# A row of offsets is added by GpSimd to the residual rows instead of by a TensorE product with ones

## The reference, cut to what matters

```python
y  = layernorm(x)                                    # without gain
y  = layernorm(y + causal_attention(y, y, y), g1, beta1)
y  = layernorm(y + attention(y, ctx, ctx), g2, beta2)
ff = relu(y @ w1 + b1) @ w2 + b2                     # 256 -> 1024 -> 256
y  = layernorm(y + ff, g3, beta3)
x  = x + y
n  = layernorm(x)
h  = silu(fp4(n) @ fp4(w_gate).T) * (fp4(n) @ fp4(w_up).T)   # 256 -> 704
x  = x + fp4(h) @ fp4(w_down).T                      # 704 -> 256
```

## Time and profile before

| | |
|---|---|
| median of 3 runs | 696.39 us |
| the profiled execution | 696.67 us, of which the span of the trace is 694.9 us |
| busy: PE, PEld, DVE, ACT, POOL | 84%, 78%, 75%, 54%, 48% of the span |
| granted TensorE clock, mean | 0.95 of full speed |
| two slots in the steady part | 74.2 us |

### The profile page before, as it was taken

How to read it: one execution, slowest core, us unless ns; L and a number is a source line. 1 busy time by engine, 2 the same in 40 slices (tenths; PEclk the granted TensorE clock), 3 DMA queues, 4 the chain that set the end, 5 groups by cost and what they waited for, 6 DMA issues and landing times.

```text
span 694.9 us, 12367 instructions
## 1 busy us (share of the span) xinstructions
PE 583.9 (84%) x3989; PEld 542.1 (78%) x3989; DVE 517.9 (75%) x1305; ACT 376.3 (54%) x763; POOL 332.8 (48%) x444
## 2 busy tenths in 40 slices
PE   2744679998999989898989899998989898888665
PEld 1634568888898889897979898888989797878564
DVE  3966546878787887878787968788778878687662
ACT  2434526566565657474737565566657574646241
POOL 2332514465544555464646454555546554544431
PEclk9965979999999999999999999999999999999785
DMA  7320000001010101010100001010100010000000
GB/s 230 108 67 0 3 30 22 17 1 46 2 54 1 47 1 54 1 45 0 53 0 22 23 15 38 0 45 0 53 1 30 1 31 9 9 8 9 8 8 15
DMA packets 18726, 19.30 MB, mean 28 GB/s; under 512 B 1520, under 2 KB 18176, under 8 KB 18688
## 3 DMA queue, kind: packets, MB, share of 16 engines
q1 hardware_dynamic: 18688, 18.82, 8.9%
HBM read 14.62 MB, written 4.19 MB: 27 GB/s over the span
## 4 chain that ended last, share of the span: by engine, by line
PE 53%; DVE 21%; issue 11%; POOL 8%; ACT 4%; DMA 1%; SPq 1%; DVEq 0%; ACTq 0%; POOLq 0%
PE R L850 6%; PE R L851 5%; PE R L852 5%; POOL hq L448 5%; PE R L762 4%; DVE ha L1216 4%; PE R L915 3%; PE R L917 3%; PE R L916 3%; DVE hs L1210 2%; PE TR L762 2%; PE O L961 2%; PE O L959 2%; PE O L960 2%; DVE st L1153 2%
## 5 line engine op out<-in xcount | busy, mean ns | idle before, releaser
L436 POOL TENSOR_TENSOR rs<-mv,neg_half 128x1 f32<-128x1 f32 (+1 forms) x112 | 70.2, 635 | 79.1 <-DVE mv L1157 78.9
L850 PE MATMUL R<-gu_hi,xqT_hi 128*128 128x352 f32 x256 | 88.2, 344 | 5.4 <-ACT xqT_hi L596 2.2
L851 PE MATMUL R<-gu_lo,xqT_hi 128*128 128x352 f32 x256 | 83.1, 325 | 0.0
L852 PE MATMUL R<-gu_hi,xqT_lo 128*128 128x352 f32 x256 | 83.0, 324 | 0.0
L442 POOL TENSOR_TENSOR hs<-hh,h_rec 128x704 f32<-128x704 f32 x32 | 50.8, 1586 | 62.2 <-DVE h_rec L1193 62.2
L590 ACT ACTIVATE w_raw<-w_raw,nm,rs 128x256 f32<-128x256 f32 x64 | 36.6, 596 | 80.3 <-DVE nm L1163 80.3
L915 PE MATMUL R<-y2T_hi,w_hi 128*128 128x256 f32 x256 | 75.1, 293 | 3.3 <-DVE y2T_lo L1293 3.3
L959 PE MATMUL O<-w_hi,hT_hi 128*128 128x256 f32 x256 | 73.7, 288 | 0.0
L960 PE MATMUL O<-w_lo,hT_hi 128*128 128x256 f32 x256 | 72.8, 284 | 0.0
L961 PE MATMUL O<-w_hi,hT_lo 128*128 128x256 f32 x256 | 72.8, 284 | 0.0
L916 PE MATMUL R<-y2T_lo,w_hi 128*128 128x256 f32 x256 | 72.4, 283 | 0.0
(11 more groups left out here) (149 smaller groups left out, 1864.7 us busy)
## 6 DMA issues: line engine op xcount, KB each, us to landing
x_in<-in_x SPq DMA_DIRECT2D x16, 256.0 KB, 2.9
x_res<-in_x SPq DMA_DIRECT2D x16, 256.0 KB, 2.8
out<-x SPq DMA_DIRECT2D x32, 128.0 KB, 1.9
hT<-in_L_xattn_w SPq DMA_DIRECT2D x2, 1024.0 KB, 7.0
ctx_rows<-in_ctx SPq DMA_DIRECT2D x16, 64.0 KB, 2.5
wd_raw<-in_L_ffn_w_down SPq DMA_DIRECT2D x1, 704.0 KB, 11.4
w_raw<-in_L_ffn_w_gate SPq DMA_DIRECT2D x1, 640.0 KB, 5.2
w_raw<-in_L_ffn_w_up SPq DMA_DIRECT2D x1, 640.0 KB, 6.7
```

Source lines behind the costliest of these rows:

```text
L436: pool.tensor_tensor(rs[i][:, t0:t0 + len(ts)], mv[i][:, t0:t0 + len(ts), 1], neg_half[:, 0:len(ts)], ALU.pow).then_inc(ln_rstd[i], 1)
L850: mm(o, xh, gu_hi[:, c, m, cols], start=(c == 0), stop=False)
L851: mm(o, xh, gu_lo[:, c, m, cols], start=False, stop=False)
L852: last = mm(o, xl, gu_hi[:, c, m, cols], start=False, stop=(c == KC - 1))
```

## The change

POOL now makes y2 in two instructions for each half: z2 * g2 as before, and then, once its own first result is written, y2 = y2 + shift2_row in place. The second waits on a new semaphore y2_gained that the first raises; the consumers wait for y2_set as before, which the second raises. TensorE's product of ones and shift_parts is gone, and so are the tiles ones and shift_parts, two memsets on POOL, two ACT instructions of 1x256 and one of DVE at the start. The first of the three products of block 0 now starts the sum.

```diff
-            pool.memset(ones[:].bitcast(F32), 1.0).then_inc(const_set, 1)
-            pool.memset(shift_parts[:].bitcast(F32), 0.0).then_inc(const_set, 1)
-            pool.wait_ge(const_set, 5)
+            pool.wait_ge(const_set, 3)
...
+            def shifted_rows(b, h, t):
+
+                wait(pool, ln_out[2], b, h, F, T, t + 1)
+                pool.tensor_tensor(y2[:, t, :], z2[:, t, :], g2_row[:], ALU.mult).then_inc(y2_gained, 1)
+                wait(pool, y2_gained, b, h, F, T, t + 1)
+                if isinstance(b, int) and HALVES * b + h == F:
+                    pool.wait_ge(shift2_set, 1)
+                pool.tensor_tensor(y2[:, t, :], y2[:, t, :], shift2_row[:], ALU.add).then_inc(y2_set, 1)
...
-                    gain_rows(b, h, F, t, 2, z2, y2, g2_row, y2_set)
+                    shifted_rows(b, h, t)
...
-                        act.wait_ge(shift2_set, 1)
-                        for p in (0, 32):
-                            act.activation(shift_parts[p:p + 1, :], shift2_row[p:p + 1, :],
-                                           ACT.Copy).then_inc(shift_hi_set, 1)
...
                 o = O[1][:, 0:D]
-                if fs[0] == 0:
-                    mm(o, ones[:], shift_parts[:], start=True, stop=False)
                 for f in fs:
                     hi, lo = hT_hi[:, f, P * t:P * (t + 1)], hT_lo[:, f, P * t:P * (t + 1)]
-                    mm(o, hi, w2_hi[:, f, :], start=False, stop=False)
+                    mm(o, hi, w2_hi[:, f, :], start=(f == 0), stop=False)
...
-                        dve.wait_ge(shift_hi_set, 2)
-                        v.tensor_tensor(shift_parts[32:33, :], shift2_row[32:33, :], f32(shift_parts[32:33, :]),
-                                        ALU.subtract).then_inc(shift_parts_set, 1)
```

More of the change, by code:

```diff
@@ L103, in layer_program @@
         shift2_row = sb("shift2_row", [P, D])
-        shift_parts = sb("shift_parts", [P, D], F32R)
-        ones = sb("ones", [P, P], F32R)
         b1_fold = sb("b1_fold", [P, FC])
@@ L186, in layer_program @@
         ident_set = sem("ident_set")
-        shift2_set, shift_hi_set, shift_parts_set = sem("shift2_set"), sem("shift_hi_set"), sem("shift_parts_set")
+        shift2_set, y2_gained = sem("shift2_set"), sem("y2_gained")
         b1_turned, b1_fold_set = sem("b1_turned"), sem("b1_fold_set")
@@ L555, in _ @@
         def _(act):
-            act.wait_ge(const_set, 5)
+            act.wait_ge(const_set, 3)
             act.wait_ge(cols_turned, 1)
@@ L815, in weights_ready @@
                     pe.wait_ge(w1_lo_set, KC)
-                    for s in (w2_hi_set, w2_lo_set, b1_fold_set, shift_parts_set):
+                    for s in (w2_hi_set, w2_lo_set, b1_fold_set):
                         pe.wait_ge(s, 1)
```

## The result

The changed kernel takes 703.41 us, the median of 20 runs (699.42 to 705.79), against 697.44 us of the kernel before, the median of 20 runs beside it (695.56 to 699.81). The ratio is 1.0076, with a 95% interval of 1.0061 to 1.0092: 5.3 us slower by the ratio, 6.0 by the two medians. The forecast was +1.4 us on the 696.39 us then known, or 697.8. The measured time lies above the forecast's range, and above rival 2 (701.3) as well.

The account below looks back on a forecast made before the run. No engine was taken as the bound by itself; work goes round between PE, DVE and POOL. Additions 1.7 + 1.7 less removal 2.0 gave +1.4 us, forecast 697.8 us, range 696 to 700.

Parts of the forecast that it names:

- rival 2: Second addition delays unscale_x and residual: in all 8 slots turn_xq late without cover, nm blocked; +4.9 us, 701.3; chance 0.20.
- The removal: Product with ones gone from PE: one 0.12 us step off the path for each half 0, 2.0 us won.
- the 12 us of the durations: Rival: PE's 32 removed products count by their full durations, 12 us go, 684 us; chance 0.01.
- rival 1: Removed product on PE wins, additions on POOL cost under 1 us: -1 to -3.9 us, say 694.4; chance 0.24.
- The first addition: Half 0's addition on POOL makes x_lift of half 0 on DVE wait 0.21 us in 8 slots: 1.7 us.
- The second addition: Half 1's addition blocks x_lift, delays unscale_x and turn_xq: 0.07 us in four looped slots, 0.35 in four written out; 1.7 us.
- the 0.3 us for nm: Part of rival 2: nm on DVE blocked by residual on POOL, another 0.3 us in each of 8 slots.
- the 74.7: Sign: two looped slots forecast at 74.2 to 74.4 us; over 74.7 us would make the forecast wrong and mean rival 2.
- the three terms: The sum's parts: first addition +1.7 us, second addition +1.7 us, removed product -2.0 us.
- the forecast's eight: Slots in which the first addition was to cost 0.21 us each: tiles 4, 6, ..., 14, 16 and 17.

## Why the prediction was wrong

**The removal: right.** 0.12 us a slot, 2.5 us by the ratio (1.4 to 3.6) against 2.0. The first product of ff2 to the second is 0.19 us, the third follows 0.12 later (390.19, 390.38, 390.50). Nothing like the 12 us of the durations came, and the additions are not free as rival 1 had it.

**The first addition: the failed step.** The prediction had it block x_lift of half 0 for 0.34 - 0.13 = 0.21 us. It had rightly placed the addition (1.06 us long, forecast 1.0), but it looked on DVE only for instructions that read two SBUF tensors, and so passed over x_norm of half 1, which stands between that h_lower and x_lift and reads one. x_norm was issued at 375.15, behind the addition (374.76), which itself stood waiting for the h_lower, and so x_norm waited until the addition had ended: 0.42 us. The bound that had been written down for this case, 0.45 us should x_lift wait for a whole addition's rest, was nearly the measured value; the value taken was half of it. In slots of h = 1 the prediction had 0, since gate_up waits for the scores there. gate_up does, but turn_xq of half 0, which PE makes ahead of the scores, isn't covered. Timeline of POOL and PE in the slot of tile 11, before

```profile
408.46 0.62 POOL L547 TENSOR_TENSOR xq<-xa,x_div 128x256 f32<-128x256 f32 x1 [1.75 <-DVE xa L1226]
409.45 0.28 PE L917 MATMUL R<-y2T_hi,w_lo 128*128 128x256 f32 x1
409.57 0.38 PE L762 MATMUL TR<-ident,xq 128*128 128x128 f32 x2
```

and after:

```profile
413.44 0.62 POOL L552 TENSOR_TENSOR xq<-xa,x_div 128x256 f32<-128x256 f32 x1 [1.02 <-DVE xa L1222]
414.02 0.28 PE L918 MATMUL R<-y2T_hi,w_lo 128*128 128x256 f32 x1
414.19 0.43 PE L763 MATMUL TR<-ident,xq 128*128 128x128 f32 x2
```

From the end of unscale_x to turn_xq it was 0.49 us (409.08 to 409.57), so PE came later than the rows. Now it is 0.13, and PE waits a little for them: the step from the product ahead of it is 0.17 us instead of 0.12, and the step to the scores behind it 0.27 instead of 0.22 (409.79 and 414.46). The kernel with only the first addition has the same two steps and pays 0.11 us in a looped slot of h = 1, 0.05 in slots 5 and 15. In sum 4.3 us against 1.7.

The Trainium skill would have told: "SBUF — State Buffer", section Who interferes with whom, lists tensor_scalar among the instructions that can take the shared pair of ports. I had cited that section for two-input instructions alone. The runs agree with the page on x_norm: 0.82 to 0.84 us when an addition is ahead, for 0.41 with its scalars from SBUF and 0.295 with constants.

**The second addition: right in what it delays, low in size.** turn_xq is 0.31 us late (forecast 0.3). But x_lift got in first by 0.07 us, and x_drop, not x_lift, was blocked. Alone the addition costs 0.8 us by the ratios, forecast 1.7; on top of the first it costs more: 7.8 - 4.3 = 3.5 us by the ratios, 5.03 - 3.00 = 2.0 in the 12 slots, where 1.0 had been forecast (4 x 0.07 + 2 x 0.35). In a looped slot of h = 0 that is 0.64 - 0.42 = 0.22 us instead of 0.07. The trace shows where: at DVE's second product of h (hh), as the prediction had it. The last product of PE that it needs and hh itself, with both additions

```profile
384.37 0.32 PE L853 MATMUL R<-gu_hi,xqT_lo 128*128 128x352 f32 x1
384.80 0.52 DVE L1165 TENSOR_TENSOR hh<-hh,R 128x352 f32<-128x352 f32 x1
```

and with the first one only:

```profile
382.48 0.32 PE L856 MATMUL R<-gu_hi,xqT_lo 128*128 128x352 f32 x1
383.08 0.52 DVE L1168 TENSOR_TENSOR hh<-hh,R 128x352 f32<-128x352 f32 x1
```

hh came 0.28 us after PE's product had ended; now it comes 0.11 after, which is also the distance in slots 4 and 14 of every kernel, where DVE stands waiting for PE. Counted from the start of gate_up, PE's product ends 0.37 us later than with the first addition only (4.69 us instead of 4.32): 0.17 of them are covered, and 0.20 are paid. The prediction counted all but 0.07 of its 0.3 as covered. The view of the line of turn counts PE's longer waits for unscale_x (us, times), with its weight loads: before

```profile
  POOL xq L547: 4.0, 4
```

and after

```profile
  POOL xq L552: 9.8, 20
```

In slots 4 to 15 there were none before; now there is one ahead of turn_xq of half 1 in each slot of h = 0.

In slots 4 and 14 the second addition costs 0.53 us upon the first, forecast 0.35. There the nm that is blocked by residual shows as well, as in the forecast's rival 2:

```profile
533.45 0.53 DVE L1159 SCALAR_TENSOR_TENSOR nm<-mv,rs 128x2 f32<-128x2 f32 x1
532.52 1.43 POOL L483 TENSOR_TENSOR w_raw<-x_res,beta_row 128x256 f32<-128x256 f32 x2
```

residual ends at 533.95, after nm was issued, and nm takes 0.53 us instead of 0.24. In the looped slots residual now ends behind the issue of nm too (384.74 against 384.56 in the slot of tile 10), the point from which rival 2 was to decide, but nm takes only 0.21 instead of 0.14 us. In neither place does it seem to cost: hh starts 0.11 us behind PE's product with nm blocked or not. So rival 2 was right that its condition would be met, and wrong on the 0.3 us for nm.

**Over the 12 slots.** Forecast 4 x 0.16 + 2 x 0.44 - 6 x 0.12 = +0.8 us; measured 5.03 - 1.39 = 3.6. Of the difference of 2.8 us, some 0.2 in each of 6 slots of h = 0 is x_norm (1.2), 0.11 in each of the 4 looped slots of h = 1 and 0.05 in the other two is turn_xq of half 0 (0.6), and what is left (1.0) is the second addition upon the first. Two looped slots take 74.69 us (353.40 to 428.09), just at the 74.7 from which the prediction was to be taken as wrong.

**The range** was narrower than the prediction's own rule for it: half or one and a half of each of the three terms, all taken the worse way, give -1.3 to +4.1 us, or 695.1 to 700.5, and not 696 to 700. The measured 703.41 us is outside of both.

What stays open is the size of the interaction: 2.7 us by the ratios (7.8 - 4.3 - 0.8), uncertain by about 2.4, and 1.4 in the 12 slots of the profiles (5.03 - 3.00 - 0.65). The race with x_lift explains some of it (0.85 us in the 12 slots came back when it was decided the other way). What the additions cost in the slots behind the 15th, where two of the forecast's eight lie, was not separated.

## What to carry to other kernels

Before GpSimd gets a piece of elementwise work, list every instruction of VectorE that it can meet, single-input ones included: the next one behind the place can wait for the whole GpSimd instruction, and pays if it is on the path. The same 32 additions cost 7.8 us in one place and nothing that the runs can tell in three others. Put it where neither engine is on the path to TensorE, here in GpSimd's wait between two long steps. A semaphore that held the additions back until VectorE's last h_lower changed nothing there (0.00 and -0.07 us in the 12 slots). Where an estimate depends on who is first by less than 0.1 us, give both outcomes a price instead of taking a value between them.

## What the runs showed of the hardware

- What is blocked seems to wait rather than run slower: x_norm and x_drop took 0.82 to 0.85 us for 0.41 or 0.42, and x_lift 0.96 for 0.41, each ending 0.15 to 0.3 us behind the 128x256 addition that blocked it. A short overlap costs little: the h_lower of 370.34 began 0.25 us before a multiplication ended and took 0.12 us longer than the one of 372.98, so that about 0.13 us were free, by this estimate.
- Which of the two comes first turned on hundredths of a us: with x_lift 0.06 or 0.07 us behind the start of the addition the addition took 1.02 to 1.05 us and x_lift 0.38; with 0.08 to 0.11 us the addition took 0.72 to 0.74 and x_lift 0.90 to 0.93.
- x_norm of 128x256 takes 0.416 us with its two scalars from SBUF and 0.295 us with constants, yet 0.83 and 0.84 us when an addition is ahead. I had not expected that the slower form is blocked too.
- An addition of 128x256 on GpSimd takes 0.73 us undisturbed, and 1.05 behind a VectorE instruction that reads SBUF. A wait of this kind counts as busy time on both engines: DVE's 12 us of new busy time are x_norm (5.9 us in 14 calls) and x_drop (6.2 us in 15), all of it waiting.
